# A graph kernel: the last gather of every second round moved from GpSimd to SyncE as single rows, and the degree count regrouped

## What is computed

```python
# layer 0
out_deg = maximum(segment_sum(ones, src), 1); t1 = x @ W1
msg = (t1[src] + x[src] * x[dst] @ W2) / (sqrt(out_deg[src]) * sqrt(out_deg[dst]))
e = where(in_cnt > 0, t1 + segment_sum(msg, dst), 0) + b
e = leaky_relu(e, 0.01); x = layernorm(x + e / max(norm(e), 1e-12))
# layer 1
xt = x @ W.T + b
x = layernorm(x + segment_sum(xt[src], dst) / (segment_sum(ones, dst) + 1))
```

## Time and profile before

| | us |
|---|---|
| median of three runs | 4003.55 (4002.74 to 4003.73) |
| the profiled execution | 4001.94 |
| its span, first to last instruction | 4000.2 |
| POOL busy / PE busy / DVE busy / ACT busy in it | 2981.7 / 3070.2 / 1870.5 / 659.9 |
| layer 0's gathers, first to last | 380.3 to 1999.4 |
| layer 1's gathers, first to last | 2028.9 to 3983.3 |
| granted TensorE clock: front, layer 0, layer 1 | 0.52, 0.83, 0.70 |

### The profile page before, as it was taken

How to read it: one execution, slowest core, us unless ns; L and a number is a source line. 1 busy time by engine, 2 the same in 40 slices (tenths; PEclk the granted TensorE clock), 3 DMA queues, 4 the chain that set the end, 5 groups by cost and what they waited for, 6 DMA issues and landing times.

```text
span 4000.2 us, 43024 instructions
## 1 busy us (share of the span) xinstructions
PE 3070.2 (77%) x10186; PEld 1873.0 (47%) x10186; DVE 1870.5 (47%) x3536; ACT 659.9 (16%) x2054; POOL 2981.7 (75%) x3146
## 2 busy tenths in 40 slices
PE   4551888778888788788867888887878888888887
PEld 4441555555555556555534343444434444343433
DVE  9995455555555555555422323232323232323233
ACT  7883111111111111111100000000000000000000
POOL 7776777777777777777757777777777777777776
PEclk5555788888888888887867676767676667677767
DMA  7878455555555555555423434343434343434343
GB/s 256 267 237 301 133 155 155 155 155 156 156 157 155 156 158 152 165 156 155 128 85 116 121 115 121 115 120 115 121 115 120 115 121 115 121 115 121 115 121 108
DMA packets 294206, 582.24 MB, mean 146 GB/s; under 512 B 60723, under 2 KB 176100, under 8 KB 294180
## 3 DMA queue, kind: packets, MB, share of 16 engines
q0 software_dynamic: 150048, 409.93, 34.9%
q1 hardware_dynamic: 131364, 159.19, 11.9%
q10 hardware_dynamic: 12768, 12.85, 0.9%
HBM read 506.27 MB, written 75.45 MB: 145 GB/s over the span
## 4 chain that ended last, share of the span: by engine, by line
POOL 65%; issue 24%; DVE 6%; ACTq 1%; PE 1%; DMA 1%; POOLq 1%; DVEq 1%; ACT 1%; SPq 0%
POOL ring L479 65%; DVE hot_space L700 6%; ACTq L577 1%; PE banks L1112 0%; DVEq L693 0%; PE banks L1138 0%; POOLq L512 0%; DMA ring<-scaled_x,idx 0%; DMA scaled_x<-big 0%; ACT dst_rel L555 0%; POOLq L476 0%; ACT big L572 0%; DVEq L738 0%; POOLq L477 0%; DMA big<-in_dst 0%
## 5 line engine op out<-in xcount | busy, mean ns | idle before, releaser
L1138 PE MATMUL banks<-ring,hot_space 128*128 128x257 f32 x6252 | 2477.3, 522 | 717.9 <-DMA ring<-scaled_x,idx 345.9
L1138 PEld LDWEIGHTS banks<-ring,hot_space 128*128 128x128 f32 x6252 | 1302.1, 241 | 1813.2 <-DMA ring<-x,idx 1028.4
L479 POOL DMA_INDIRECT ring<-x,idx x1563 | 1478.7, 946 | 505.3 <-issue 475.7
L479 POOL DMA_INDIRECT ring<-scaled_x,idx x1281 | 1229.2, 960 | 408.9 <-issue 407.9
L855 DVE SCALAR_TENSOR_TENSOR big<-banks,here_mask,big 128x257 f32 x784 | 343.3, 479 | 1710.4 <-PE banks L1138 1710.4
L811 DVE TENSOR_TENSOR hot_space<-banks,dst_rel 128x1024 f32<-128x1024 f32 x395 | 483.4, 1224 | 183.4 <-issue 179.1
L593 ACT COPY idx<-src_col 128x8 int32 (+1 forms) x392 | 77.2, 197 | 2238.2 <-PE banks L1138 2238.2
L489 POOL DMA_INDIRECT ring<-in_x,src_col x276 | 264.0, 957 | 84.1 <-issue 84.1
L555 ACT ACTIVATE dst_rel<-columns,halves 128x128 bf16<-128x128 f32 (+1 forms) x896 | 254.2, 374 | 36.9 <-PE banks L1051 32.8
L1044 PE MATMUL banks<-hot_space 128*128 128x98 bf16 x1120 | 104.2, 282 | 141.2 <-DVE hot_space L700 141.2
L1112 PE MATMUL banks<-w_s,a_t 128*128 128x256 f32 x784 | 185.4, 391 | 0.0
(11 more groups left out here) (115 smaller groups left out, 1169.9 us busy)
## 6 DMA issues: line engine op xcount, KB each, us to landing
kept_rows<-ring SPq DMA_DIRECT2D x94, 384.0 KB, 3.2
ring<-kept_rows SPq DMA_DIRECT2D x47, 768.0 KB, 5.6
ring<-x,idx POOLq DMA_INDIRECT x1563, 2.7
ring<-scaled_x,idx POOLq DMA_INDIRECT x1281, 2.8
dst_col<-in_src SPq DMA_DIRECT2D x47, 384.0 KB, 6.2
scaled_x<-big ACTq DMA_DIRECT2D x14, 896.0 KB, 15.9
x<-out_t SPq DMA_DIRECT2D x98, 128.0 KB
x_t<-x SPq DMA_DIRECT2D x98, 128.0 KB, 2.1
```

Of the source, the lines that this page charges most:

```text
L479: g.indirect_dma_start(ring[:, u, 0:D], None, table[layer], bass.IndirectOffsetOnAxis(ap=idx[:, u:u + 1], axis=0)).then_inc(rows_in[u], 16)
L1138: last = nc.tensor.matmul(group_sum(k % SUMS), dst_hot[:, k % HOTS, u - k * GT, :], ring[:, u, 0:DW], start=u == tiles[0], stop=u == tiles ...
```

## The change

In layer 0 and in layer 1, for the rounds 3, 5, ... 47 (23 of them a layer, h = 1 to 23 with round 2h+1), POOL no longer gathers the last tile of the round (place 31). SP gathers it instead, into a buffer of its own (`hand_rows`, in the space of `src_lo`): it loads the tile's 128 source numbers from DRAM (`load_hand_src`), reads 32 of them at a time into registers, and issues one DMA of one row for each (`hand_part`, four parts). When all have landed and PE has finished round 2h, SP copies the buffer to place 31 of the ring by one DMA (`pass_hand`), and waits for its landing before it overwrites the buffer (`hand_free`). PE waits for that copy's semaphore in these rounds. SP's loop runs over two rounds now. Its x loads and its stores, together in `next_pair` before, are apart (`next_x`, `store_pair`) with a part of 32 rows between them.

In the front, STEP_TILES goes from 448 to 480 and SB from 4 to 7, with two buffers in place of three: ACT makes 68 batches of 7 tiles and one of 4; DVE makes 68 hist batches in place of 70; PE alternates hist batch and step batch.

```diff
-SB = 4
-STEP_BATCHES = 112
-STEP_TILES = STEP_BATCHES * SB
+SB = 7
+STEP_BATCHES = 69
+STEP_TILES = 480
...
+            def hand_part(layer, h, part, load_next=False):
+                if part == 0:
+                    sp.wait_ge(hand_src_in, 16 * hand_no(layer, h))
+                    sp.sem_inc(sync_turn, 1)
+                first = part * HAND_ROWS
+                _, rows = nc.values_load_multi_w_load_instructions(
+                    hand_src[:, first:first + HAND_ROWS], engines=[mybir.EngineType.SP], min_val=0, max_val=NODES - 1,
+                    skip_runtime_bounds_check_because="a source is a node's number, as for the gathers")
+                if load_next:
+                    load_hand_src(h + 1)
+                for n, row in enumerate(rows):
+                    sp.dma_start(hand_rows[first + n:first + n + 1, :],
+                                 table[layer][bass.ds(row, 1), :]).then_inc(hand_in[layer], 16)
+            def pass_hand(layer, h):
+                sp.wait_ge(hand_in[layer], 16 * P * h)
+                sp.sem_inc(sync_turn, 1)
+                sp.wait_ge(groups_done, group_no(layer, 2 * h, GR - 1) + 1)
+                sp.dma_start(ring[:, HAND_U, 0:D], hand_rows).then_inc(hand_over, 16)
+            def hand_free(layer, h):
+                sp.wait_ge(hand_over, 16 * hand_no(layer, h))
+                sp.sem_inc(sync_turn, 1)
...
+                    with sp.Fori(1, HANDS - 1) as h:
+                        hand_part(layer, h, 2)
+                        next_x(layer, 2 * h - 2)
+                        if layer == 0:
+                            load_kept(2 * h + 1)
+                            load_places(2 * h + 2)
+                        hand_part(layer, h, 3, load_next=True)
+                        store_pair(layer, 2 * h - 2)
+                        pass_hand(layer, h)
+                        hand_free(layer, h)
+                        hand_part(layer, h + 1, 0)
+                        next_x(layer, 2 * h - 1)
+                        if layer == 0:
+                            load_kept(2 * h + 2)
+                            load_places(2 * h + 3)
+                        hand_part(layer, h + 1, 1)
+                        store_pair(layer, 2 * h - 1)
...
-                    with g.Fori(LOOP_FIRST, LOOP_END) as i:
-                        for q in range(4):
-                            gather_quarter(layer, i, q, first=0 if layer else KEPT)
+                    with g.Fori(1, HANDS) as h:
+                        for half in range(2):
+                            for q in range(4):
+                                gather_quarter(layer, 2 * h + half, q, U - half, 0 if layer else KEPT)
...
+                        elif u == HAND_U and not (isinstance(i, int) and i < 2):
+                            pe.wait_ge(rows_in[u], 16 * (layer * (HANDS + 1) + (i >> 1) + 2))
+                            if not (isinstance(i, int) and i < 3):
+                                pe.wait_ge(hand_over, 16 * (layer * (HANDS - 1) + (i - 1 >> 1)))
```

More of the change, by code:

```diff
@@ L238, in gnn @@
         gather_turn = sem("gather_turn")
+        hand_src_in = sem("hand_src_in")
+        hand_in = [sem(f"hand_in{n}") for n in range(2)]
+        hand_over = sem("hand_over")
         sync_turn = sem("sync_turn")
@@ L404, in _ @@
                         load_x(layer, 0, s, s)
+                    load_hand_src(1)
                     if layer == 0:
@@ L547, in _, with step_batch @@
             nc.scalar.copy(idx[:, :], src_col[:, 0:U]).then_inc(idx_ready, 4)
-            def step_batch(n, third):
+            def step_batch(n, half, tiles=SB):
                 act.wait_ge(steps_used, n + 1)
                 act.sem_inc(act_turn, 1)
-                for t in range(SB):
+                for t in range(tiles):
                     for digit, (first, size) in enumerate(((0, P), (P, HI))):
-                        last = nc.scalar.activation(steps[:, third, t, first:first + size], columns[:, 0:size], ACT.Sign,
+                        last = nc.scalar.activation(steps[:, half, t, first:first + size], columns[:, 0:size], ACT.Sign,
                                                     bias=step_digits[:, digit, bass.ds(n * SB + t, 1)], scale=-1.0)
@@ L559, in _ @@
             act.wait_ge(step_digits_made, 1)
[L560 to L564, removed]
+            with act.Fori(0, STEP_BATCHES // 2) as b:
+                for half in range(2):
+                    step_batch(2 * b + half, half)
+            step_batch(STEP_BATCHES - 1, 0, STEP_TILES - (STEP_BATCHES - 1) * SB)
             act.wait_ge(degree_ready, 1)
@@ L1046, in hist_batch, with step_batch @@
                 last.then_inc(hot_used, 1)
-            def step_batch(n, third, first, last_one):
+            def step_batch(n, half, first, last_one, tiles=SB):
                 pe.wait_ge(steps_made, n + 1)
-                for t in range(SB):
-                    last = nc.tensor.matmul(step_sums, steps[:, third, t, 0:P], steps[:, third, t, P:P + HI],
-                                            start=first and t == 0, stop=last_one and t == SB - 1)
+                for t in range(tiles):
+                    last = nc.tensor.matmul(step_sums, steps[:, half, t, 0:P], steps[:, half, t, P:P + HI],
+                                            start=first and t == 0, stop=last_one and t == tiles - 1)
                 last.then_inc(steps_used, 1)
@@ L1067, in span @@
                     hist_batch(2 * n + half, half, first and half == 0, False)
-                    for third in ((0, 1), (2,))[half]:
-                        step_batch(3 * n + third, third, first and third == 0, False)
+                    step_batch(2 * n + half, half, first and half == 0, False)
             span(0, True)
@@ L1073, in _ @@
                 span(n, False)
-            for k in range(SRC_BATCHES // 2 * 3, STEP_BATCHES):
-                step_batch(k, k % 3, False, k == STEP_BATCHES - 1)
+            step_batch(STEP_BATCHES - 1, 0, False, True, STEP_TILES - (STEP_BATCHES - 1) * SB)
             pe.wait_ge(step_diffs_made, 1)
@@ L1160, in _ @@
                     round_(layer, 1, True, with_kept=first, find=first)
-                    with pe.Fori(LOOP_FIRST, KEPT_ROUNDS) as i:
+                    round_(layer, 2, True, with_kept=first, find=first)
+                    with pe.Fori(3, KEPT_ROUNDS) as i:
                         round_(layer, i, True, with_kept=first, find=first)
```

49 lines of the change are left out of this document (33 added, 16 removed).

## The result

The changed kernel takes 4209.65 us (median, 4207.57 to 4210.53), the kernel before beside it 4003.6 (4002.74 to 4003.73). The ratio is 1.0515, 95% interval 1.0502 to 1.0527: 206 us slower, where I had forecast 141. The profiled execution took 4210.53 us with a span of 4208.5, 208.3 us more than before.

What follows compares the result with a forecast made beforehand. The prediction took the kernel to be bound by POOL's gathers. From the profiled 4001.9 us, plus 177 (layer 0), minus 28.8 (layer 1), minus 8 (front), it got 4142, as a median 4144 us; range 3935 to 4450.

Steps and rivals of the forecast that it cites:

- the forecast's own sign: In the profile afterwards: if a load of 32 registers on SP is not near 1.2 us, the forecast's size is wrong.
- The bound and the budgets: POOL's gathers, about 1.25 us each, set the pace; SP's loop may take 64.4 us in layer 0, 78.8 in layer 1.
- A row: SP's single-row DMA with computed address: 0.243 + 0.20 = 0.44 us, 56.7 us for 128 rows (bounds 36 and 71).
- The register loads: SP's four loads of 32 registers: 4 x 1.22 = 4.9 us for two rounds (bounds 1.2 and 38.9).
- The old work and the new small parts: SP's loop, two rounds: previous work 7.7 us (3.0 less in layer 1); source load, copy and two landings 4.1 us.
- How the loop becomes time: Layer 0: SP's loop of 73.4 us against 65.7 before, charged for all 23 repetitions: 177 us lost.
- What is late behind SP: Layer 0's x loads come some 4 us late; once slack is gone, mix, PE's sums, index refill and POOL follow SP.
- The count: In the front, the count ends at about 291 us instead of 307.7; 8 us gained at the first table gather.
- The copy and the bytes: PE's wait for the copy at tile 31 and about 1% more DMA share cost nothing.
- A (SP keeps up): Rival: SP keeps up in both layers, layer 0's loop within 64.4 us; 3938 us, chance 0.30.
- C (registers one by one): Rival: registers load one after the other, SP paces both layers; 5516 us at the upper bound, 4628 at half; chance 0.22.
- D (one DMA engine): Rival: single rows load one DMA engine, 15 us of two rounds, only lengthening landings; no chance of its own.

Runs made afterwards that it cites:

- the layer-1 run 28 by itself: The changed kernel with SP's single rows in layer 1 only, layer 0 as before: 3963.86 us, ratio 0.9904; 28 is microseconds gained, not a run number.
- both runs that stay under it: The changed kernel with 64 two-row DMAs a tile (3933.27 us), and with one register loaded per part, all 32 DMAs fetching that row (3934.4 us).
- the run with one number: The changed kernel with each register load reading one source number instead of 32, all 32 DMAs of the part fetching that row: 3934.4 us, ratio 0.9828.
- the hint: The changed kernel with one instruction more at the top of SP's loop, hinting that its closing branch will be taken: 4134.28 us, ratio 1.0327.
- the run with two loads: The changed kernel with each part's 32 registers loaded twice, each load serving 16 rows (368 loads instead of 184): 4470.74 us, ratio 1.1173.
- the run with short rows: The changed kernel with each of the 128 single-row DMAs fetching 64 bytes of its row instead of 1024: 4209.76 us, ratio 1.0518.

## Why the forecast came out as it did

The direction and the mechanism were right: SP paces layer 0 and POOL layer 1, so that layer 0 loses more than layer 1 and the front gain. The size was 65 us too small (206 measured, 141 forecast), and by the forecast's own sign, a load of registers not near 1.2 us, the size was wrong. That it was not further off is partly luck: the rows were 3.1 us a pass too dear, the loads 3.5 too cheap, the closing of the loop (3.3) was missing, and too many passes were charged.

**The bound and the budgets**: right. A gather off POOL is worth about 1.25 us where POOL sets the pace: layer 1 gave 28 us of 28.8, and the layer-1 run 28 by itself. The budget of 64.4 us for two rounds of layer 0 is the loop measured in both runs that stay under it (64.48 and 64.38).

**A row**: 0.42 us against 0.44 (0.41 from row to row within a part), from a single-row DMA of the trace and the gap between computed ones. Both pieces were a little too high: the DMA takes 0.229 where I took 0.243, and the register work with its gaps 0.19 where I took 0.20. Of 128 rows that is 3.1 us.

**The register loads**: this was named the least certain term, and it was one of the two steps with wrong reasoning. I took SP's one row of 1.216 us for one register as the price of 32, since both bounds came from loads of one. The traces have 2.05 us for 32 and, in the run with one number, 0.46 for one, so the 1.216 can't have been the steady price of one register; it was the first load on that engine, and what made it dear was not looked into. The error was 3.3 us a pass, 3.5 with the gaps. The Trainium skill, page "Runtime: NRT & Kernel Launch", section "Instruction fetch mechanics", has about 200 ns for each register even in bulk. Here the measurement decides against it: 0.051 us for each further register, from SBUF, and 0.46 for the first. The estimate of 25.6 us for the four loads would be 3 times too high.

**The branch**: missing from the sum. I added up the instructions of the loop and none for its closing. The stop behind it is 3.1 us a pass with the long body, under 0.3 with half the rows (64 DMAs a pass), and 0.2 with the hint, which gave 75 us in all. This is the largest part of what the loop's sum lacked, since the errors of the rows and the loads nearly cancel. The same section of that page of the Trainium skill says that a taken branch whose target is not in the window of two pages forces a fetch before execution goes on. The runs agree with it in kind: the stop is there with the long bodies, where the instruction queue has 261 packets, and not with the short ones, with 24. I had used the section for its number on registers and not for this sentence.

**The old work and the new small parts**: right. The old work takes 7.9 us a pass against 7.7. The source load, the copy and the landings take 4.65 against 4.1; 2.5 of them are SP's stop for the copy's landing, and SP hardly waits for the last row's.

**How the loop becomes time**: I charged all 23 repetitions, and 240.3 / 11.9 = 20.2 came. That POOL's lead would absorb "a few of 23 at most" was right. So the forecast's own sum with the measured loop gives 23 x 11.9 = 274 us where 240 were lost. The loop was 4.2 us too short, which is 97 us by 23, and 34 us too many were charged for; the two explain, with 4 us from the change of layers and the tail and 1 from layer 1, the 68 us between the forecast's 4142 and the profiled 4210.5.

**What is late behind SP**: right in kind. SP's waits for var_ready have left layer 0's loop (49.0 us, 4 times). The x loads are what reaches the others: mix (360 us of waits), PE's turn (726), index copies and POOL (294). The late stores reach DVE too: it stands 167 us in 44 times before finishing a pair (line 948). What I did not see is the chain from x load to var_ready of 28.5 us, with the store's landing in it, which decides where the parts of rows may stand.

**The count**: 8.0 us of 8, with the count's end at 289.3 against 291 forecast. **The copy and the bytes**: nothing, as forecast.

**The rivals**: A (SP keeps up) was excluded by 13.2 us of loop (77.6 against 64.4). C (registers one by one) was wrong by its price, but the run with two loads shows its mechanism. D (one DMA engine) was excluded by the run with short rows for the bytes, and by SP's 3.0 us of waits for the rows' landings in layer 0.

## What to carry to other kernels

When work moves to a queue that runs in fixed order, add up every instruction of that queue's loop, the register loads and the closing branch too, and compare it with the time that the pace-setting engine leaves for it; here a microsecond over cost 22, and a microsecond under nothing. A tile moved gave 1.2 to 1.5 us wherever the loop stayed under its budget, so ask for as much moved work as fits (one tile in four rounds in layer 0, one in two in layer 1; one in three in layer 0 was not run) and not for the most. And spread the moved work evenly between the transfers that others wait for: the same instructions in another order cost 98 us.

## What the chip showed that I had not expected

SP issues a DMA of one row with an address from a register every 0.41 us, of which the DMA instruction is 0.228; a DMA of two rows takes 0.42 us (6.66 for 16), so half as many DMAs take half the time. A load of registers from SBUF took 0.46 us for one and 2.05 for 32. Behind a backward branch over 128 rows of three instructions each SP stood 3.1 us at each pass, over 64 such rows 0.25, and over the long body with the hint 0.18. And PE's busy time fell from 3070 to 2809 us with the same 10186 matmuls, while the kernel got slower; so here its busy time did not tell which kernel was faster, and why it fell no run shows.
